# A cross-attention and mixture-of-experts layer on one core: the order of its tail laid out anew

## The chip, the cores and the metric

The kernel runs on one core of a Trainium2 chip. The metric is device time in microseconds (us) of one execution; lower is better. TensorE (PE) does matrix products and transposes, VectorE (DVE) and ScalarE (ACT) do elementwise work, GpSimd (POOL) does small work and issues the indirect DMAs, SyncE (SP) issues the other DMAs. Each engine runs its own list of instructions in order and waits on semaphores.

## What is computed

Two batches of 512 tokens of width 256, with a context of 1024 tokens each. First cross-attention with 16 heads, then a feed-forward layer made of a shared expert and eight routed experts, of which every token takes the best two.

```
x = x + attention(layernorm(x), ctx, ctx)           # W_Q, W_K, W_V, W_O, biases
xf = layernorm(x)
shared_out = silu(xf @ sw1) * (xf @ sw3) @ sw2       # 256 -> 512 -> 256
s = sigmoid(xf @ router_w.T)                         # 8 experts
topk_idx = top_k(s + router_bias, 2)                 # gates: s at the two, over their sum
routed_out = sum over the two of gate * gelu(xf @ ew1[e]) @ ew2[e]   # 256 -> 256 -> 256
out = x + shared_out + routed_out
```

## The kernel before, in words

One list, `steps`, is built in Python (line 84 on). TensorE, VectorE and ScalarE each walk the whole list and emit what a step asks of them, so the list is the order of the work on all three. SyncE and GpSimd have hand-written orders of their own. Products of float32 quality are made of three products of high and low parts (`product`, L1155), so an operand is split after each transpose: ScalarE copies the high part out of PSUM, VectorE subtracts it to get the low part.

Up to about 245 us the steps are attention units. The work on the routing of batch 0 (norm, transposes, logits, `router`, `choose`, `rank`, `place`, `gates`) is put beside the last units by `around_unit`. The tail begins behind them. What it holds, for batch b:

- Routing. `stats2`, `var2`, `norm2`: second layer norm (a first guess of 1/sqrt comes from GpSimd). `xpose2`: transposes of the normalised tokens. `logits`: 24 small matmuls. `router` (L916 to L923, with Exp on ScalarE at L851): sigmoid. `choose` (L930 to L938): the two best experts as one-hots, 12 small VectorE operations. `rank` (L1430 to L1434): matmuls that count tokens per expert. `place` (L992 to L1010): the row of each token in the sorted order (semaphore `pos_ready` at L1006), then the expert of each tile (`texp_ready` at L1010). `gates` (L943 to L956).
- Sorting. On GpSimd `sort_x(b)` (L693) writes the tokens into `xs_d` in HBM, sorted by expert: eight indirect DMAs. SyncE's `load_xs(b, i)` (L494) reads them back in pieces (`LOADS`), after all eight have landed.
- Expert tiles. 15 tiles of 128 rows, in 8 groups of two (the last of one). Groups are numbered q = 0 to 7 for batch 0 and 8 to 15 for batch 1. A group has four steps: `tx` (transposes of x, L1244; copies L782, L1033), `th` (12 matmuls with the first expert weights; Gelu L787), `tt` (transposes, L1265; copies L792, L1037), `ty` (12 matmuls with the second weights; copy to `ys`, L797). They form a pipeline: one round does `tx` of q, `th` of q-1, `tt` of q-2, `ty` of q-3. The results wait in a ring of `YR` buffers until GpSimd's `scatter_y(q)` (L698) has written them to their tokens in HBM (`ys_d`).
- Shared expert. `h` p = 0 to 3 for batch 0 and 4 to 7 for batch 1: 12 matmuls of 128x512 each, Silu on ScalarE (L773), three VectorE operations (L969, L975, L976). `y` (b, t), t = 0 to 3: 12 matmuls of 128x256 each; `add_y` (L982) adds the result to `x_sb`. `h`, `y`, `oproj`, `xpose2`, `logits` and `rank` take turns in two PSUM slots (the ring, `ring_at`).
- The end. SyncE loads the scattered results (L528, `yk`) when all of a batch have landed, `combine` (b, i) multiplies them with the gates and adds them (L1019), SyncE stores half a batch at a time (L532).

`with_group` says which routing and shared steps follow which round of the tiles. ScalarE's functions Exp, Silu and Gelu are in different tables; a switch shows as ACT_TABLE_LOAD. VectorE's routing operations are each followed by a wait on their own end (`link`).

Of the kernel before, what the change touches and what calls it, by code (L numbers as in the profile page):

```python
# [1479 lines left out]
```

## Time and profile before

| | |
|---|---|
| median of 3 runs | 373.58 us (371.82 to 375.38) |
| the profiled execution | 370.11 us, of which the span is 368.4 us |
| PE busy | 329.1 us (89%) |
| DVE busy | 260.7 us (71%) |
| ACT busy | 228.6 us (62%) |
| POOL busy | 150.2 us (41%) |
| chain that ended last, by engine | PE 66%, DVE 12%, DMA 7%, ACT 6%, issue 4%, POOL 2% |
| mean granted TensorE clock | 0.97 |

Busy time is the time in which an engine worked. The chain is followed back from the last instruction, at each step to what released it. The granted clock is the share of TensorE's full 2.4 GHz; half is 1.2 GHz. An interval in brackets behind a row is idle time of the engine before it, and what ended that.

### The profile page before, as it was taken

To read this page: it belongs to the slowest core of one execution; us is meant where nothing else is said; L and a number is where in the kernel's file an instruction comes from. 1 tells how busy PE (TensorE), PEld (TensorE's weight loads), DVE (VectorE), ACT (ScalarE), POOL (GpSimd) and SP (SyncE) were. 2 spreads that over 40 slices of the span, in tenths; PEclk is the share of its full clock that TensorE was granted. 3 is DMA by queue.
4 is the path that set the end of the run, shared out by engine and by line. 5 is a ranking of instruction groups with operands and counts; after the bars stand their busy time and mean duration, and the time that the engine had idled before them with its cause. 6 is when DMAs were issued, how large, how long until landed. Compare 5 with 4: busy or idle time off the path is not lost.

```text
span 368.4 us, 7264 instructions
## 1 busy us (share of the span) xinstructions
PE 329.1 (89%) x2636; PEld 202.5 (55%) x2636; DVE 260.7 (71%) x424; ACT 228.6 (62%) x408; POOL 150.2 (41%) x210
## 2 busy tenths in 40 slices
PE   5878998999999999999999999997999497599990
PEld 2665565333333333333643444467999495599880
DVE  6766988999999999999679538449642456355314
ACT  6452445898899899999568867631544352355710
POOL 5032479021063453466644645830131245515450
PEclk9998999999999999999999999999998899699997
DMA  7679990033160605436197050126020112663124
GB/s 287 255 247 347 303 371 9 2 112 126 43 196 6 217 21 158 138 86 210 28 322 204 19 163 3 56 73 204 3 101 26 47 45 86 200 217 142 59 73 171
DMA packets 29563, 49.52 MB, mean 134 GB/s; under 512 B 6404, under 2 KB 19844, under 8 KB 27844
## 3 DMA queue, kind: packets, MB, share of 16 engines
q1 hardware_dynamic: 27320, 43.02, 36.4%
q0 software_dynamic: 2208, 6.04, 4.6%
q8 instruction: 22, 0.36, 0.4%
q14 instruction: 13, 0.11, 0.1%
HBM read 29.00 MB, written 17.33 MB: 126 GB/s over the span
## 4 chain that ended last, share of the span: by engine, by line
PE 66%; DVE 12%; DMA 7%; ACT 6%; issue 4%; POOL 2%; SPq 1%; DVEq 0%; POOLq 0%; ACTq 0%
PE psum L1155 21%; PE psum L1334 18%; PE psum L1209 14%; PE psum L1215 7%; DVE negm L1046 3%; ACT PB L760 2%; PE psum L1244 2%; POOL xs_d L693 2%; PE psum L1265 2%; DMA VA<-xs_d 1%; DMA PB<-in_ctxT_dram 1%; SPq L425 1%; DMA PB<-ys_d 1%; DVE x_sb L1019 1%; DMA qs_d<-SWH 1%
## 5 line engine op out<-in xcount | busy, mean ns | idle before, releaser
L1046 DVE TENSOR_REDUCE negm<-psum 128x1 f32<-128x1024 f32 x128 | 153.7, 1222 | 13.9 <-PE psum L1215 13.3
L760 ACT ACTIVATE PB<-psum 128x512 f32<-128x512 f32 x256 | 138.4, 598 | 27.6 <-PE psum L1209 18.9
L1334 PE MATMUL psum<-PB,VA 128*17 128x256 f32 x1024 | 79.8, 385 | 2.8 <-ACT TMP L818 2.1
L1155 PE MATMUL psum<-EWT,WH 128*128 (+1 forms) x408 | 67.1, 316 | 2.0 <-DVE WH L1037 1.6
L1155 PEld LDWEIGHTS psum<-EWT,WH 128*128 128x128 f32 x408 | 57.2, 203 | 5.9 <-issue 4.1
L1209 PE MATMUL psum<-EWT 64*128 64x512 f32 x160 | 58.6, 449 | 0.4 <-ACT PB L760 0.2
L1215 PE MATMUL psum<-EWT 64*128 64x512 f32 x160 | 54.1, 457 | 4.4 <-DMA EWT<-qs_d 2.8
L698 POOL DMA_INDIRECT ys_d<-VA x30 | 28.9, 965 | 42.7 <-ACT VA L797 37.2
L1334 PEld LDWEIGHTS psum<-PB,VA 128*17 128x17 f32 x1024 | 17.4, 95 | 46.2 <-issue 34.8
L1209 PEld LDWEIGHTS psum<-EWT 64*128 64x128 f32 x160 | 24.5, 184 | 30.7 <-ACT PB L760 23.6
L1215 PE MATMUL psum<-S 64*128 64x512 f32 x96 | 32.2, 457 | 1.7 <-DVE negm L1046 1.1
L1209 PE MATMUL psum<-S 64*128 64x512 f32 x96 | 32.5, 463 | 0.0
L1215 PEld LDWEIGHTS psum<-EWT 64*128 64x128 f32 x160 | 22.0, 187 | 8.2 <-DMA EWT<-qs_d 3.0
L1155 PE MATMUL psum<-XT,SWH 128*128 128x512 f32 x96 | 25.0, 401 | 0.0
L782 ACT ACTIVATE WH<-psum 128x512 fp32r<-128x512 f32 (+1 forms) x16 | 9.1, 569 | 24.4 <-PE psum L1244 24.3
L1209 PEld LDWEIGHTS psum<-S 64*128 64x128 f32 x96 | 13.3, 184 | 17.8 <-ACT PB L760 13.9
L1037 DVE TENSOR_TENSOR WH<-psum,WH 128x512 fp32r<-128x512 f32 (+1 forms) x16 | 10.5, 658 | 16.4 <-ACT WH L792 16.4
L624 POOL TENSOR_TENSOR EWT<-RAW,EWT 128x512 fp32r<-128x512 f32 x16 | 20.6, 1288 | 1.3
L1155 PEld LDWEIGHTS psum<-XT,SWH 128*128 128x128 f32 x96 | 17.2, 188 | 6.3 <-issue 3.4
L797 ACT ACTIVATE VA<-psum 128x512 f32<-128x512 f32 (+1 forms) x16 | 9.1, 572 | 15.0 <-PE psum L1155 15.0
L787 ACT ACTIVATE RAW<-psum 128x512 f32<-128x512 f32 (+1 forms) x16 | 9.1, 571 | 12.3 <-PE psum L1155 12.2
L621 POOL TENSOR_SCALAR EWT<-RAW 128x512 fp32r<-128x512 f32 x16 | 9.9, 617 | 16.3 <-DMA RAW<-in_ew_dram 10.6
(189 smaller groups left out, 442.6 us busy)
## 6 DMA issues: line engine op xcount, KB each, us to landing
ks_d<-SWH SPq DMA_DIRECT2D x8, 512.0 KB, 4.4
RAW<-in_ew_dram SPq DMA_DIRECT2D x16, 256.0 KB, 3.0
xs_d<-VA SPq DMA_DIRECT2D x2, 1927.5 KB, 13.3
EWT<-ks_d SPq DMA_DIRECT2D x15, 256.0 KB
EWT<-qs_d SPq DMA_DIRECT2D x30, 128.0 KB
S<-ks_d SPq DMA_DIRECT2D x9, 256.0 KB
S<-qs_d SPq DMA_DIRECT2D x18, 128.0 KB
qs_d<-SWH SPq DMA_DIRECT2D x4, 512.0 KB, 4.8
```

The source lines that it names most:

```text
L621: pool.tensor_scalar(hi, RAW[:, c % 2, :], 1.0, 1.0, ALU.mult, ALU.mult).then_inc(pool_chain, 1)
L624: pool.tensor_tensor(lo, RAW[:, c % 2, :], raw(hi), ALU.subtract).then_inc(w_split, 1)
L698: pool.indirect_dma_start(ys_d[q // NGR], bass.IndirectOffsetOnAxis(sidx[:, q // NGR, i:i + 1], 0), ys[q % YR][:, j * D:(j + 1) * D], None ...
L760: act.activation(PB[:, n % PR, i * N:(i + 1) * N], bank[t % 3], ACT.Exp, scale=DK ** -0.5).then_inc(exp_done, 1)
L782: act.activation(xb[q % 2][0][:, 0:w], bank[0][:, 0:w], ACT.Copy).then_inc(x_hi, 1)
L787: act.activation(hs[q % 2][:, 0:w], bank[1][:, 0:w], ACT.Gelu).then_inc(gelu_done, 1)
L1037: dve.tensor_tensor(lo[:, 0:w], bank[2][:, 0:w], raw(hi[:, 0:w]), ALU.subtract).then_inc(h_lo, 1)
L1046: dve.tensor_reduce(negm[:, g % 2, r // QT, r % QT:r % QT + 1], psum[:, k0:k0 + 2, :].rearrange("p a n -> p (a n)"), AX.X, ALU.max, negate ...
L1155: r = pe.matmul(dst, a_hl[u], b_hl[v], start=first and i == 0, stop=last and i == 2)
L1209: pe.matmul(bank[t % 3], KS[s][rows, j, kp * P:(kp + 1) * P], QS[s][rows, j, :], start=True, stop=True).then_inc(scores_done, 1)
L1215: return pe.matmul(ring_bank(("max", m), half), QS[s][rows, j, qt * P:(qt + 1) * P], KS[s][rows, j, :], start=True, stop=True)
L1334: last = pe.matmul(acc[32 * j:32 * j + DK + 1, cols], VA[:, b, kp + KP * kk, GH * hg + j, :], PB[:, (4 * q + j) % PR, kk * N:(kk + 1) * N] ...
```

## The change

The tail's order is written out step by step instead of by `with_group`. The parts:

- `choose` and `place` are cut in two steps each, the last four operations of `place` become a step of their own (`experts`), and all of them are put between the tile steps of batch 0, `router` behind `add_y` and ahead of `th` 4. The logits of batch 1 are put between tile steps too. `norm2` of batch 1 comes ahead of `tx` 2 and `tt` 0.
- A step `exp_table` runs Exp on a scratch value ahead of the logits, so ScalarE changes tables there.
- `tx` 0 comes ahead of `oproj` and its wait for `oproj` is gone; `y` (0, 0) comes right behind `oproj`.
- `h` 7 goes from the eighth round of batch 1 to a place between `tx` 8 and `tx` 9; `h` 5 and `h` 6 follow `ty` 7.
- All four `y` of batch 1 come behind `ty` 15. Two used to stand between `ty` 14 and `ty` 15. `add_y` is cut in two halves; for batch 1 the second half comes behind both `combine`, and is the last operation.
- `combine` of batch 0 comes one round later.
- `LOADS`: four pieces instead of three, of 2, 2, 4 and 7 tiles. The loads of batch 1 wait until the low parts of x of batch 0 are made (`x_lo`), not until its results are scattered.
- `YR` 6 instead of 4; GpSimd scatters three groups ahead of `sort_x(1)` instead of four.

The same arithmetic is done. `choose` and `place` of batch 0 get the new cuts too.

```
@@ -40,10 +40,10 @@
-YR = 4
+YR = 6
...
-LOADS = ((0, 2), (2, XV), (XV, NTL))
+LOADS = ((0, 2), (2, 4), (4, XV), (XV, NTL))
...
-        for at, kind in ((18, "router"), (20, "choose"), (22, "rank"), (23, "place"), (25, "gates")):
+        for at, kind in ((18, ("router", 0)), (20, ("choose", 0, 0)), (20, ("choose", 0, 1)), (22, ("rank", 0)),
+                         (23, ("place", 0, 0)), (23, ("place", 0, 1)), (24, ("experts", 0)), (25, ("gates", 0))):
             if r == at:
-                todo += [(kind, 0)]
+                todo += [kind]
...
-    steps += [("sums", NG - 1), ("norm", NG - 1), ("oproj_part", 1), ("h", 2), ("h", 3), ("oproj", 1)]
-    with_group = {(0, 0): [("stats2", 1, t) for t in range(4)] + [("var2", 1)],
-                  (0, 1): [("y", 0, 0)], (0, 2): [("norm2", 1), ("y", 0, 1)], (0, 3): [("y", 0, 2), ("xpose2", 1)],
-                  (0, 4): [("y", 0, 3)] + [("logits", 1, t) for t in range(4)], (0, 5): [("router", 1)],
-                  (0, 6): [("choose", 1), ("rank", 1)], (0, 7): [("place", 1)], (0, 8): [("h", 4), ("gates", 1)],
-                  (0, 9): [("h", 5)], (0, 10): [("h", 6)],
-                  (1, 3): [("combine", 0, 0)], (1, 4): [("combine", 0, 1)], (1, 7): [("h", 7)],
-                  (1, 9): [("y", 1, 0), ("y", 1, 1)], (1, 10): [("y", 1, 2), ("y", 1, 3)]}
-    for b in range(B):
-        for i in range(NGR + 3):
-            steps += [(kind, NGR * b + i - d) for d, kind in enumerate(("tx", "th", "tt", "ty")) if 0 <= i - d < NGR]
-            steps += with_group.get((b, i), [])
-    steps += [("combine", 1, 0), ("combine", 1, 1)]
+    steps += [("sums", NG - 1), ("norm", NG - 1), ("oproj_part", 1), ("h", 2), ("h", 3), ("tx", 0), ("oproj", 1)]
+    steps += [("y", 0, 0), ("th", 0)] + [("stats2", 1, t) for t in range(4)] + [("var2", 1)]
+    steps += [("tx", 1), ("y", 0, 1), ("th", 1), ("norm2", 1), ("tx", 2), ("tt", 0), ("y", 0, 2)]
+    steps += [("th", 2), ("tx", 3), ("xpose2", 1), ("tt", 1), ("y", 0, 3), ("ty", 0), ("th", 3), ("exp_table",)]
+    steps += [("logits", 1, 0), ("tx", 4), ("logits", 1, 1), ("tt", 2), ("logits", 1, 2), ("ty", 1), ("add_y", 0, 0)]
+    steps += [("add_y", 0, 1), ("logits", 1, 3), ("router", 1), ("th", 4), ("choose", 1, 0), ("tx", 5), ("choose", 1, 1)]
+    steps += [("tt", 3), ("ty", 2), ("th", 5), ("rank", 1), ("place", 1, 0), ("tx", 6), ("place", 1, 1), ("tt", 4)]
+    steps += [("ty", 3), ("th", 6), ("tx", 7), ("tt", 5), ("ty", 4), ("experts", 1), ("th", 7), ("tt", 6), ("ty", 5)]
+    steps += [("h", 4), ("tt", 7), ("ty", 6), ("ty", 7), ("gates", 1), ("h", 5), ("h", 6)]
+    steps += [("tx", NGR), ("h", 7), ("tx", NGR + 1), ("th", NGR)]
+    for i in range(2, NGR + 3):
+        q = NGR + i
+        for kind, r in (("tx", q), ("th", q - 1), ("tt", q - 2), ("ty", q - 3)):
+            if NGR <= r < 2 * NGR:
+                steps.append((kind, r))
+        if i in (4, 5):
+            steps.append(("combine", 0, i - 4))
+    steps += [("y", 1, 0), ("y", 1, 1), ("add_y", 1, 0), ("combine", 1, 0), ("y", 1, 2), ("y", 1, 3)]
+    steps += [("combine", 1, 1), ("add_y", 1, 1)]
...
-        ys = [va[1][:, i * N:(i + 1) * N] for i in range(YR)]
+        ys = [va[1][:, i * N:(i + 1) * N] for i in range(4)] + [TMP[:, i, :] for i in range(2)]
...
-                    for q in range(lo // 2, (hi + 1) // 2):
-                        sp.wait_ge(ys_stored[q % YR], ys_count(q))
+                    sp.wait_ge(x_lo, (hi + 1) // 2)
...
-                for q in range(NGR * b + NGR - YR, NGR * b + NGR):
+                for q in range(max(0, NGR * b + NGR - YR), NGR * b + NGR):
...
-            for q in range(4):
+            for q in range(3):
                 scatter_y(q)
             sort_x(1)
-            for q in range(4, 2 * NGR):
+            for q in range(3, 2 * NGR):
...
-                    elif q == 0:
-                        act.wait_ge(ring_full, ring_at[("oproj", 1)] + 1)
...
+                elif st[0] == "exp_table":
+                    act.activation(exp_in[:, :], exp_in[:, :], ACT.Exp)
...
-            def add_y(tb):
-                ring_wait(("y", tb))
-                for t in range(4):
-                    src = ring_bank(("y", tb), t // 2)[:, (t % 2) * D:(t % 2 + 1) * D]
+            def add_y(tb, half):
+                if half:
+                    ring_wait(("y", tb))
+                else:
+                    dve.wait_ge(y_half, tb + 1)
+                for t in range(2 * half, 2 * half + 2):
+                    src = ring_bank(("y", tb), half)[:, (t % 2) * D:(t % 2 + 1) * D]
                     dst = x_sb[:, 4 * tb + t, :]
                     last = dve.tensor_tensor(dst, src, dst, ALU.add)
-                last.then_inc(slot_empty(("y", tb)), 1)
-                dve.wait_ge(*freed(("y", tb)))
-            def place(b):
+                if half and tb:
+                    last.then_inc(combined, 1)
+                elif half:
+                    last.then_inc(slot_empty(("y", tb)), 1)
+                    dve.wait_ge(*freed(("y", tb)))
+                else:
+                    link(last)
...
-                    if k == 0:
+                    if k == 0 or (b, i) == (1, 1):
                         link(last)
-                last.then_inc(combined, 1)
+                if (b, i) != (1, 1):
+                    last.then_inc(combined, 1)
...
-                    if t == 3:
+                    if t == 1:
+                        r.then_inc(y_half, 1)
+                    elif t == 3:
```

On VectorE, at the router of batch 1 (`xn` holds the routing's small tiles here, `WH` a tile's low part): before.

```order
L1031 TENSOR_TENSOR VA<-PB,spare 128x2
L1033 TENSOR_TENSOR WH<-psum,WH 128x512
L1037 TENSOR_TENSOR WH<-psum,WH 128x512
L916 COPY xn<-psum 128x32
L918 COPY rs<-xn 128x1
L921 TENSOR_SCALAR xn<-xn 128x32
L922 RECIPROCAL xn<-xn 128x32
L923 TENSOR_TENSOR xn<-xn,rows 128x32
L1031 TENSOR_TENSOR VA<-PB,spare 128x2
L1033 TENSOR_TENSOR WH<-psum,WH 128x512
L1037 TENSOR_TENSOR WH<-psum,WH 128x512
L930 TENSOR_REDUCE rs<-xn 128x4
```

The same place after the change (L923 is now the copy out of PSUM, L1056 a tile's low part).

```order
L994 TENSOR_TENSOR x_sb<-psum,x_sb 128x256 x4
L923 COPY xn<-psum 128x32
L925 COPY rs<-xn 128x1
L928 TENSOR_SCALAR xn<-xn 128x32
L929 RECIPROCAL xn<-xn 128x32
L930 TENSOR_TENSOR xn<-xn,rows 128x32
L937 TENSOR_REDUCE rs<-xn 128x4
L938 TENSOR_TENSOR xn<-xn,rs 128x32
L939 TENSOR_TENSOR xn<-xn,desc 128x32
L940 TENSOR_REDUCE rs<-xn 128x4
L941 TENSOR_TENSOR xn<-xn,rs 128x32
L944 SCALAR_TENSOR_TENSOR xn<-xn 128x32
```

Before, the router's copy stood behind the low parts of `tx` 5 and `tt` 3, and the choice behind those of `tx` 6 and `tt` 4. After, both follow the logits directly, and the low part of `tx` 5 comes behind the first half of the choice.

On TensorE, where batch 0 ends and batch 1 begins: before (12 matmuls of 128x512 are one `h`, here `h` 6).

```order
L1155 MATMUL psum<-EWT,WH 128x256 x2
L1155 MATMUL psum<-XT,SWH 128x512 x12
L1225 TENSOR_LOAD VA
L1244 MATMUL psum<-ident,VA 128x128 x4
L1225 TENSOR_LOAD VA
```

After: `h` 5 and `h` 6, `tx` 8, `h` 7, `tx` 9.

```order
L1180 MATMUL psum<-XT,SWH 128x512 x24
L1250 TENSOR_LOAD VA
L1269 MATMUL psum<-ident,VA 128x128 x4
L1180 MATMUL psum<-XT,SWH 128x512 x12
L1250 TENSOR_LOAD VA
L1269 MATMUL psum<-ident,VA 128x128 x4
```

`h` 7 now stands between the first two transposes of batch 1; it was some 30 us further down.

On VectorE, the end of the program: before.

```order
L1037 TENSOR_TENSOR WH<-psum,WH 128x512
L1037 TENSOR_TENSOR WH<-psum,WH 128x256
L982 TENSOR_TENSOR x_sb<-psum,x_sb 128x256 x4
L1019 SCALAR_TENSOR_TENSOR x_sb<-PB,VA,x_sb 128x256 x8
L179 UNCONDITIONAL_BRANCH
```

After.

```order
L1060 TENSOR_TENSOR WH<-psum,WH 128x256
L994 TENSOR_TENSOR x_sb<-psum,x_sb 128x256 x2
L1041 SCALAR_TENSOR_TENSOR x_sb<-PB,VA,x_sb 128x256 x8
L994 TENSOR_TENSOR x_sb<-psum,x_sb 128x256 x2
L186 UNCONDITIONAL_BRANCH
```

Two of the four additions of the shared expert's result moved behind the combination.

## Rows read from the trace of the kernel before

**Rows 1.** The page: span, and the granted TensorE clock in 40 slices.

```profile
span 368.4 us, 7264 instructions
PEclk9998999999999999999999999999998899699997
```

**Rows 2.** Windows: length, busy per engine (PE, PEld, DVE, ACT, POOL), PEclk, DMA share, GB/s.

```profile
277.00:283.00 6.00, 6.00 (x40) 6.00 (x40) 1.70 (x5) 1.91 (x4) 0.00 (x0) 0.72 0.07 25
...
312.00:323.00 11.00, 5.54 (x26) 4.86 (x26) 3.33 (x7) 4.00 (x6) 5.93 (x7) 0.69 0.63 186
```

**Rows 3.** Timeline of TensorE, steady stretch: start, duration, line, [idle before <- releaser].

```profile
263.51 0.60 PE L1244 MATMUL psum<-ident,VA 128*128 128x128 f32 x4
263.86 1.68 PE L1155 MATMUL psum<-EWT,WH 128*128 x12
265.38 0.60 PE L1265 MATMUL psum<-ident,RAW 128*128 128x128 f32 x4
265.74 1.67 PE L1155 MATMUL psum<-EWT,WH 128*128 x12
267.25 1.60 PE L1155 MATMUL psum<-SWH,S 128*128 128x256 f32 x12
268.69 1.04 PE L1373 MATMUL psum<-ident,xn 128*128 128x128 f32 x8
```

**Rows 4.** Timeline of TensorE: its waits in the tail, and its slow steps.

```profile
256.43 0.63 PE L1244 MATMUL psum<-ident,VA 128*128 128x128 f32 x4 [1.87 <-DVE WH L1033]
...
277.76 2.75 PE L1155 MATMUL psum<-EWT,WH 128*128 x12
...
291.33 0.19 PE L1430 MATMUL psum<-VA,lower 128*128 128x8 bf16 x2 [4.75 <-DVE VA L938]
...
292.06 2.91 PE L1155 MATMUL psum<-EWT,WH 128*128 x12
...
308.30 0.98 PE L1155 MATMUL psum<-EWT,WH 128*128 x6 [1.63 <-DVE WH L1037]
...
315.31 0.99 PE L1244 MATMUL psum<-ident,VA 128*128 128x128 f32 x4 [3.27 <-DMA VA<-xs_d]
318.30 1.11 PE L1244 MATMUL psum<-ident,VA 128*128 128x128 f32 x4 [1.99 <-DMA VA<-xs_d]
319.06 2.91 PE L1155 MATMUL psum<-EWT,WH 128*128 x12
...
350.17 0.41 PE L1265 MATMUL psum<-ident,RAW 128*128 128x128 f32 x2 [1.11 <-DVE WH L1037]
...
355.55 3.04 PE L1155 MATMUL psum<-SWH,S 128*128 128x256 f32 x24
```

**Rows 5.** Timeline of VectorE: the router's copy, and the end of `place`.

```profile
282.64 0.18 DVE L916 COPY xn<-psum 128x32 f32<-128x32 f32 x1
...
298.69 0.17 DVE L1006 CAST VA<-xn 128x8 int32<-128x8 f32 x1
```

**Rows 6.** Timeline of ScalarE: the load of the Exp table.

```profile
283.50 1.28 ACT L851 ACT_TABLE_LOAD   x1
```

**Rows 7.** Timeline of GpSimd: first and last scatter of the sort, the last results.

```profile
299.14 0.96 POOL L693 DMA_INDIRECT xs_d<-xn,VA  x1 [8.00 <-DVE VA L1006]
...
309.90 0.96 POOL L693 DMA_INDIRECT xs_d<-PB,VA  x1 [2.20 <-issue]
...
356.40 0.96 POOL L698 DMA_INDIRECT ys_d<-VA  x1 [1.16 <-ACT VA L797]
```

**Rows 8.** Chain of waits in order of time, its end: start, duration, what.

```profile
356.40 2.40 DMA ys_d<-VA
...
358.94 3.35 DMA PB<-ys_d
```

**Rows 9.** Timeline of VectorE: the last additions and the combination of batch 1.

```profile
358.62 1.42 DVE L982 TENSOR_TENSOR x_sb<-psum,x_sb 128x256 f32<-128x256 f32 x4 [7.16 <-PE psum L1155]
362.39 3.51 DVE L1019 SCALAR_TENSOR_TENSOR x_sb<-PB,VA,x_sb 128x256 f32<-128x256 f32 x8 [2.35 <-DMA PB<-ys_d]
```

More of the change, by code:

```diff
@@ L355, in xattn_ffn @@
         combined = sem("combined")
+        y_half = sem("y_half")
         x_turned = sem("x_turned")
@@ L923, in route, with choose @@
                 link(dve.tensor_tensor(sel_, s_, bc(rbv), ALU.add))
-            def choose(b):
-                if b == 0:
+            def choose(b, k):
+                if b == 0 and k == 0:
                     dve.wait_ge(pv_done, 4 * HG * KP)
@@ L934, in first_max @@
                     link(dve.tensor_tensor(oh, w_, bc(per_token(b, 1)), ALU.is_equal))
-                first_max(oh)
-                link(dve.scalar_tensor_tensor(out=sel_, in0=oh, scalar=-1e30, in1=sel_, op0=ALU.mult, op1=ALU.add))
-                first_max(oh2)
-                dve.tensor_tensor(both_b[:, :, :], oh, oh2, ALU.add).then_inc(both_ready, 1)
+                if k == 0:
+                    first_max(oh)
+                    link(dve.scalar_tensor_tensor(out=sel_, in0=oh, scalar=-1e30, in1=sel_, op0=ALU.mult, op1=ALU.add))
+                else:
+                    first_max(oh2)
+                    dve.tensor_tensor(both_b[:, :, :], oh, oh2, ALU.add).then_inc(both_ready, 1)
             def gates(b):
@@ new lines, in add_y, with cube @@
+                if half and tb:
[3 more added lines that the diff above has]
+                    dve.wait_ge(*freed(("y", tb)))
+                else:
+                    link(last)
+            last1 = lambda v, n: v.rearrange("p (a o) -> p a o", o=1).broadcast_to([P, v.shape[1], n])
+            mid1 = lambda v, n: v.rearrange("p (o a) -> p o a", o=1).broadcast_to([P, n, v.shape[1]])
+            def cube(b, lo, a, n):
+                return work[b][:, lo:lo + a * n].rearrange("p (a n) -> p a n", n=n)
@@ new lines, in place @@
+            def place(b, part):
+                w = work[b]
+                tiles, first, rk, base = w[:, 320:328], w[:, 328:336], w[:, 344:384], w[:, 480:512]
+                if part == 0:
+                    if b == 0:
+                        dve.wait_ge(order_consts, 15)
+                    ring_wait(("rank", b))
+                    dve.tensor_copy(rk, ring_bank(("rank", b))[:, 0:40]).then_inc(slot_empty(("rank", b)), 1)
+                    dve.wait_ge(*freed(("rank", b)))
+                    link(dve.tensor_tensor(cube(b, 384, NE, 4), last1(rk[:, 32:40], 4), mid1(steps128[:, :], NE), ALU.is_gt))
+                    link(dve.tensor_reduce(tiles, cube(b, 384, NE, 4), AX.X, ALU.add))
+                    link(dve.tensor_tensor(cube(b, 416, NE, NE), before[:, :, :], mid1(tiles, NE), ALU.mult))
+                    link(dve.tensor_reduce(first, cube(b, 416, NE, NE), AX.X, ALU.add))
+                else:
+                    link(dve.scalar_tensor_tensor(out=base.rearrange("p (t e) -> p t e", e=NE), in0=mid1(first, 4),
+                                                  scalar=float(P), in1=rk[:, 0:32].rearrange("p (t e) -> p t e", e=NE),
+                                                  op0=ALU.mult, op1=ALU.add))
+                    link(dve.tensor_tensor(cube(b, 0, 2, 4 * NE), chosen(b), twice(base), ALU.mult))
+                    link(dve.tensor_reduce(tiles_f(b), cube(b, 0, 8, NE), AX.X, ALU.add))
+                    dve.tensor_copy(pos[:, b, :], tiles_f(b)).then_inc(pos_ready, 1)
@@ L1007, in place, with experts @@
+            def experts(b):
+                w = work[b]
+                tiles, first, ends, over = w[:, 320:328], w[:, 328:336], w[:, 336:344], w[:, 464:464 + NTL]
                 link(dve.tensor_tensor(ends, first, tiles, ALU.add))
-                link(dve.tensor_tensor(cube(344, NTL, NE), last1(column[:, 0:NTL], NE), mid1(ends, NTL), ALU.is_ge))
-                link(dve.tensor_reduce(w[:, 464:464 + NTL], cube(344, NTL, NE), AX.X, ALU.add))
-                dve.tensor_scalar(texp[:, b, :], w[:, 464:464 + NTL], float(NE - 1), float(EXPERT), ALU.min, ALU.mult)\
+                link(dve.tensor_tensor(cube(b, 344, NTL, NE), last1(column[:, 0:NTL], NE), mid1(ends, NTL), ALU.is_ge))
+                link(dve.tensor_reduce(over, cube(b, 344, NTL, NE), AX.X, ALU.add))
+                dve.tensor_scalar(texp[:, b, :], over, float(NE - 1), float(EXPERT), ALU.min, ALU.mult)\
@@ L1138, in _ @@
                     hidden(st[1])
-                elif st[0] == "y" and st[2] == 3:
-                    add_y(st[1])
+                elif st[0] == "add_y":
+                    add_y(*st[1:])
                 elif st[0] == "choose":
-                    choose(st[1])
+                    choose(*st[1:])
                 elif st[0] == "place":
-                    place(st[1])
+                    place(*st[1:])
+                elif st[0] == "experts":
+                    experts(st[1])
                 elif st[0] == "gates":
```

20 lines of the change are left out of this document (removed).

## The prediction

> **What bounds the kernel now.** I read the page first. Over most of the 368.4 us span the granted clock stands at nine tenths or more; it dips only in slices near 280, 295 and 315 us [rows 1]. Up to about 255 us the change touches nothing but the cut of batch 0's routing, so the question lies in the last 115 us. There the timeline of TensorE is an almost unbroken row of steps, and the end follows its pace wherever it is unbroken. From starts that follow each other, a step costs at full clock: `tx` 0.35 us (263.51 to 263.86), `th` 1.52, `tt` 0.36, `ty` 1.51, `y` 1.44 [rows 3]. What isn't work is in the idle times of the same timeline [rows 4]: 1.87 (VectorE's low part of `tx` 0), 4.75 (`rank` waits for the choice), 1.63 (`ty` 7 waits for a low part behind the gates), 3.27 and 1.99 (the first two loads of batch 1), 1.11 (`tt` 15). The third thing is slow steps: `th` 4, `th` 6 and `th` 8 take 2.75, 2.91 and 2.91 us where 1.68 is the rule [rows 3, 4]; in 277 to 283 us and in 312 to 323 us the granted clock is 0.72 and 0.69 [rows 2], that is, part of these stretches ran at 1.2 GHz. The last two dips follow TensorE's waits; the first follows the 24 tiny logits matmuls.
>
> Why the loads are late is one chain. The router's copy on VectorE runs at 282.64 although the logits end near 277.5, for it stands behind two tile steps [rows 5]. Exp then waits for a table load of 1.28 [rows 6]. Choice, rank and place follow, each behind further tile steps, and the positions are there at 298.87 [rows 5]. The sort takes from 299.14 to 310.86 on GpSimd [rows 7], and batch 1's first transpose starts at 315.31 [rows 4]: 16.4 us after the positions. While this goes on TensorE runs out of batch 0.
>
> **The change, part by part.** I walk TensorE through the new list with the prices above.
>
> *Start.* `tx` 0 ahead of `oproj` makes no time: `y` (0, 0) now stands behind `oproj` and needs its slot, which VectorE frees by the same additions as before. The wait is again about 1.9 us, ending near 256.4, and `tx` 0, `tx` 1, `th` 0, `y` (0, 0) are done at about 259.8 in both. From there to the end of the logits the list holds the same steps in another order; with VectorE's part in it I find one wait of 0.3 (`th` 1 for its low part, `y` (0, 1) doesn't cover it whole). So the logits end at 277.7, as before within 0.4.
>
> *Routing of batch 1.* The copy goes from 282.64 to 277.8. Router: 1.4 us instead of 3.2, the Exp table being there since `exp_table`. Twelve operations of the choice at 0.22 each are 2.7, the low part of `tx` 5 between them 0.85 and its wait 0.25: 282.9. `rank` 0.6, five operations of `place` at 0.23 1.2, low part of `tx` 6 0.8, four operations 0.9: the positions at 286.4, 12.5 us earlier than 298.87. On TensorE this costs short waits, as the low parts of `tx` 5 and `tx` 6 come late behind a half of the choice or of `place`: 0.2 for `th` 5, 0.1 for `th` 6. Without such cover the dearest piece is 1.3. The 4.75 go, since `th` 4, `tx` 5, `tt` 3, `ty` 2 and `th` 5 now lie between logits and `rank`.
>
> A rule bears on this. The trace shows 1.28 for a table load and the function right behind it [rows 6]. The Trainium skill (ScalarE: Activation LUTs, What ACT_TABLE_LOAD costs) adds a drain of about 1.38 to each switch. By the rule the Gelu table's load behind the router's Exp would hold back `th` 4's Gelu, and with it `tx` 5's copy and `rank`, 1.4 us longer; the sum below would be 1.4 us less good. I go by the row.
>
> *Sort and loads.* GpSimd has its three groups scattered by 284.7. With 16.4 from positions to landed data, the first piece lands at 302.9. When is TensorE there? It reached `tx` 8 at 315.31; minus waits of 4.75 + 1.63 + 3.27, minus slow steps of about 4.0 ahead of it, plus waits of its own (0.3 + 0.2 + 0.1, and 1.4 for `ty` 7, whose low part is behind `h` 4's three operations on VectorE), plus 0.8 for a clock that still dips: 304.5. So the load is 1.6 us early and TensorE isn't held. The second piece, now two tiles, is covered by `h` 7: the 1.99 go. Nearest rows for the other pieces: 8 tiles took some 5.4 us before; the last seven are wanted 10 us after `tx` 8.
>
> *Clock.* Twelve-matmul steps lose 1.07, 1.23 and 1.23 [rows 3, 4]; the transposes beside them 0.39 and 0.5 (0.99 and 1.11 against 0.60), further small ones about 1.1: 5.5 in all, 4.0 ahead of `th` 8, 1.5 from it on. Two of the three dips follow waits that go. For the one behind the logits I keep half, 0.8: they are as tiny as before (the bound 1.6), but tile steps stand between them (the bound 0).
>
> *Batch 1.* New waits: 0.3 before `tx` 9 and 1.25 before `tx` 10 (the low part of `tx` 9 stands behind `h` 7's 1.8 us on VectorE), 0.65 before `ty` 15, which needs `ty` 14's PSUM bank copied out and has no `y` in between any more. Gone: 0.2, the 1.11, one table pair, and two `y`, 2.88, from ahead of `ty` 15. `h` 7 itself is only moved.
>
> *End.* Before, the last group's scatter starts at 356.40, lands 2.40 later, `yk` takes 3.35 [rows 8], the combination 3.51 [rows 9], and the span ends 2.5 later. After, groups 13, 14 and 15 leave TensorE faster than GpSimd issues (1.27 per tile), so the last scatter starts 2.1 late against `ty` 15. The four `y` take 5.8 behind `ty` 15 and hide in the 9 us of scatter and load. The second `add_y` half is now last on VectorE: half of 1.42, 0.7 [rows 9].
>
> *Nothing.* Six `ys` buffers, the later `combine` and the split `place` of batch 0: `ty` never waited for a buffer, and batch 0's routing has tens of microseconds to spare. `yk` of batch 0 needs nine scatters behind the sort (to 309.8, landed 312, loaded 316), and VectorE wants it at 322.
>
> **Sum.** Waits gone 4.75 + 1.63 + 3.27 + 1.99 + 0.2 + 1.11 = 12.95; clock 5.5; two `y` 2.9: 21.3. Against it waits 0.3 + 0.2 + 0.1 + 1.4 + 0.3 + 1.25 + 0.65 = 4.2, clock 0.8, end 2.8: 7.8. Net 13.5 less: span 354.9, with the 1.7 around it 356.6. The profiled execution (370.11) lies 3.5 under the median 373.58; carried over, 360.1. I say 360.
>
> **Rivals.**
> 1. *The waits go but the clock doesn't come back.* For: the first dip began in a stretch without a wait [rows 2]. Against: 323 to 343 us ran full, and new waits are below 1.9, like the one at 256.43, after which steps were at full speed [rows 3, 4]. Then 4.7 of the sum are missing: 364.8. The Trainium skill (TensorE: Matmul & The Clock Gate, The HAM clock gate) calls the slow phase run-variable and advises against fitting a count to it. By this the 4.7 I credit are the least safe term. The trace agrees in that its three dips have no common length.
> 2. *Transfers replace waits.* The first load, or batch 0's `yk`, comes late: the sort, the backlog of nine scatters and 2 MB of loads now run close together, and `combine` (0, 0) holds VectorE and so TensorE. For: the slack of the first load is only 1.6. Against: the same mix ran in 312 to 323 us with DMA at 0.63 [rows 2]. A loss of 4: 364.
> 3. *Better than walked.* Waits are half of mine, the clock stays up, the end's queue is hidden: 3.5 more, 356.5.
> 4. *The routing pieces starve TensorE* (the other side). It happens between 278 and 287 us: every piece on VectorE holds a low part, TensorE idles in each round, and the clock halves the 12 us of work there. Price: 6 of waits, 6 of clock, and the first load late by as much, 3: within 1%, 371 to 375. It turns into a loss only if the positions come after about 303, that is 16 us later than walked; for that VectorE, 5 us busy in 10 there, would have to be full twice over.
>
> That the change doesn't do what it says is excluded by the instruction order.
>
> **Chances.** Forecast 0.60, clock 0.12, transfers 0.12, better 0.11, starving 0.05 (of it slower 0.02). The forecast's own range is 356.5 to 363.5, from new waits between 2 and 6, the dip 0 to 1.6, and the median's offset between 2 and 5. To hold 8 in 10 I reach over rivals 1 and 2 and part of 3: 355 to 366.5. A difference below 1% can't be told from none here. Faster by over 1%: 0.95, within 0.03, slower 0.02.
>
> **What would show it.** Positions near 286 us and the sort's first scatter right behind; `tx` 8 without idle time before it, near 304.5; `h` 7, then `tx` 9 at once; `rank` without its 4.75; `th` 6 and `th` 8 at 1.68; `ty` 15 ending near 338; the last scatter 3 us after it, queued behind its neighbours; `add_y` last. Wrong if `tx` 8 waits for a load, if `th` 4 to `th` 8 stay near 2.9, or if the end after `ty` 15 takes more than 17 us.

## The result and the profile after

The changed kernel takes 359.65 us (median of 4 runs, 356.12 to 361.89) against 372.98 us before in the same job: ratio 0.960, 95% interval 0.951 to 0.970. The prediction said 360 and kept 355 to 366.5. The profiled execution took 356.12 us with a span of 354.3 us; the sum had said 356.6 and 354.9. With the later jobs there are 16 executions of the changed kernel, from 355.4 to 364.6, median 360.7. The ratios leave out executions that lie more than 1.5% above the fastest of their kernel; medians are over all executions.

The page of the changed kernel: the span, and the clock in 40 slices, which has no dip before the last slice, against [rows 1].

```profile
span 354.3 us, 7265 instructions
PEclk9999999999999999999999999999999999999996
```

The timeline of TensorE, its waits in the tail and the steps around them. L1180 is now the product helper, L1269 `tx`, L1290 `tt`.

```profile
255.89 1.69 PE L1180 MATMUL psum<-SWH,S 128*128 128x256 f32 x12 [1.81 <-DVE x_sb L1158]
...
261.08 1.69 PE L1180 MATMUL psum<-EWT,WH 128*128 x12 [0.19 <-DVE WH L1056]
...
277.40 1.68 PE L1180 MATMUL psum<-EWT,WH 128*128 x12
...
282.07 1.69 PE L1180 MATMUL psum<-EWT,WH 128*128 x12 [0.68 <-DVE WH L1056]
...
298.68 0.98 PE L1180 MATMUL psum<-EWT,WH 128*128 x6 [1.37 <-DVE WH L1060]
299.49 5.61 PE L1180 MATMUL psum<-XT,SWH 128*128 128x512 f32 x24
304.94 0.60 PE L1269 MATMUL psum<-ident,VA 128*128 128x128 f32 x4
305.30 2.99 PE L1180 MATMUL psum<-XT,SWH 128*128 128x512 f32 x12
308.47 0.63 PE L1269 MATMUL psum<-ident,VA 128*128 128x128 f32 x4 [0.18 <-DVE WH L1056]
308.85 1.67 PE L1180 MATMUL psum<-EWT,WH 128*128 x12
311.65 0.63 PE L1269 MATMUL psum<-ident,VA 128*128 128x128 f32 x4 [1.13 <-DVE WH L1056]
...
336.34 1.69 PE L1180 MATMUL psum<-EWT,WH 128*128 x12 [0.40 <-ACT VA L802]
338.90 0.98 PE L1180 MATMUL psum<-EWT,WH 128*128 x6 [0.88 <-ACT VA L802]
339.72 5.91 PE L1180 MATMUL psum<-SWH,S 128*128 128x256 f32 x48
```

The 4.75 before `rank`, the 3.27 and 1.99 before the two loads, and the slow steps of 2.75 and 2.91 [rows 4] are gone: `th` 4 (277.40) takes 1.68 and `th` 8 (308.85) 1.67. `tx` 8 starts at 304.94 right behind `h` 6, ten microseconds earlier than the 315.31 of before.

The timeline of VectorE: the router's copy and the end of `place`, against [rows 5].

```profile
278.22 0.19 DVE L923 COPY xn<-psum 128x32 f32<-128x32 f32 x1
...
287.03 0.17 DVE L1025 CAST VA<-xn 128x8 int32<-128x8 f32 x1
```

The timeline of GpSimd: first and last scatter of the sort, the first scatter of group 14, the last scatter of all, against [rows 7]. And the end of the chain of waits, against [rows 8].

```profile
287.73 0.97 POOL L700 DMA_INDIRECT xs_d<-xn,VA  x1 [3.17 <-DVE VA L1025]
...
298.34 0.97 POOL L700 DMA_INDIRECT xs_d<-PB,VA  x1 [2.06 <-issue]
...
338.93 0.96 POOL L705 DMA_INDIRECT ys_d<-VA  x1 [0.33 <-ACT VA L802]
...
341.46 0.96 POOL L705 DMA_INDIRECT ys_d<-VA  x1 [0.30 <-issue]
```

```profile
341.46 2.40 DMA ys_d<-VA
...
344.01 3.40 DMA PB<-ys_d
```

The positions come 11.7 us earlier and the sort follows them at once. Take the start of the first step behind the wait for the `oproj` additions on VectorE (255.89; before it is 256.43 [rows 4], where the low part of `tx` 0, behind the additions, ends the wait). From there to the end of the span there were 112.0 us, now 98.4: 13.6 less. The other 0.5 fell ahead of the tail.

The executions of one kernel differ by several microseconds with the mean granted clock: the changed kernel's lie between a span of 353.7 at 0.991 and 362.9 at 0.961. A single profile is therefore compared from a point behind its dips. The measure below is **th 1 to end**, from the start of `th` 1 of batch 0 to the end of the span. It is 93.2 in the changed kernel (354.3 less 261.08), and 93.3 and 93.5 in two more profiles of it. It can't be read finer than about 0.5: the load of `yk` near the end alone takes 3.4 to 4.0 in the profiles of the changed kernel and its variants, though no edit touches it.

Five of the experiments have only two executions each (medians 360.94 for the two `y`, 367.35 for the ring of four, 360.85 without `exp_table`, 365.24 for the logits, 359.01 for three loads). That is too few to settle differences of 1 to 4 us, so they are read by their profiles, one each.

### The profile page after: what moved, and what is told of

Read it like the earlier page. It is cut to its first block, busy times and chain, and to the rows that moved or that the text cites. A ratio compares the mean times of both kernels' runs of the same rounds, so it can differ in the third digit from the quotient of the medians.

```text
span 354.3 us, 7265 instructions
## 1 busy us (share of the span) xinstructions
PE 322.7 (91%) x2636; PEld 196.3 (55%) x2636; DVE 260.8 (74%) x424; ACT 226.0 (64%) x407; POOL 150.8 (43%) x210
## 4 chain that ended last, share of the span: by engine, by line
PE 66%; DVE 16%; ACT 6%; DMA 6%; issue 3%; SPq 1%; POOL 1%; DVEq 0%; POOLq 0%; ACTq 0%
PE psum L1180 23%; PE psum L1359 17%; PE psum L1234 13%; PE psum L1240 7%; DVE negm L1069 6%; ACT PB L767 2%; DMA PB<-in_ctxT_dram 2%; PE psum L1290 1%; PE psum L1269 1%; DVE PB L978 1%; DMA EWT<-qs_d 1%; DVE S L985 1%; DMA PB<-ys_d 1%; DVE x_sb L1041 1%; DMA qs_d<-SWH 1%
## 5 line engine op out<-in xcount | busy, mean ns | idle before, releaser
L1180 PE MATMUL psum<-EWT,WH 128*128 (+1 forms) x408 | 62.4, 302 | 4.5 <-DVE WH L1060 1.4
L1180 PEld LDWEIGHTS psum<-EWT,WH 128*128 128x128 f32 x408 | 53.3, 190 | 8.9 <-issue 7.4
L1359 PEld LDWEIGHTS psum<-PB,VA 128*17 128x17 f32 x1024 | 17.4, 95 | 46.2 <-issue 34.9
L705 POOL DMA_INDIRECT ys_d<-VA x22 | 21.4, 973 | 30.3 <-ACT VA L802 26.0
L1180 PE MATMUL psum<-XT,SWH 128*128 128x512 f32 x96 | 24.9, 401 | 0.0
L1234 PEld LDWEIGHTS psum<-S 64*128 64x128 f32 x96 | 13.3, 184 | 17.8 <-ACT PB L767 14.3
L1180 PEld LDWEIGHTS psum<-XT,SWH 128*128 128x128 f32 x96 | 17.2, 188 | 6.4 <-issue 3.4
L792 ACT ACTIVATE RAW<-psum 128x512 f32<-128x512 f32 (+1 forms) x16 | 9.1, 571 | 18.0 <-PE psum L1180 17.8
L571 POOL TENSOR_TENSOR rstd<-ve,mhalf 128x4 f32<-128x4 f32 x4 | 4.6, 1152 | 28.6 <-DVE ve L876 28.6
L675 POOL TENSOR_TENSOR TMP<-TMP 128x512 f32<-128x512 f32 x6 | 7.7, 1281 | 20.1 <-ACT TMP L837 20.1
```

What stands on the lines that cost most here:

```text
L675: pool.tensor_tensor(RC, U[g % 2], RC, ALU.mult).then_inc(rc_scaled, 1)
L705: pool.indirect_dma_start(ys_d[q // NGR], bass.IndirectOffsetOnAxis(sidx[:, q // NGR, i:i + 1], 0), ys[q % YR][:, j * D:(j + 1) * D], None ...
L792: act.activation(hs[q % 2][:, 0:w], bank[1][:, 0:w], ACT.Gelu).then_inc(gelu_done, 1)
L1180: r = pe.matmul(dst, a_hl[u], b_hl[v], start=first and i == 0, stop=last and i == 2)
L1234: pe.matmul(bank[t % 3], KS[s][rows, j, kp * P:(kp + 1) * P], QS[s][rows, j, :], start=True, stop=True).then_inc(scores_done, 1)
L1359: last = pe.matmul(acc[32 * j:32 * j + DK + 1, cols], VA[:, b, kp + KP * kk, GH * hg + j, :], PB[:, (4 * q + j) % PR, kk * N:(kk + 1) * N] ...
```

## The experiments

### The routing put back late

```
-    ... ("th", 3), ("exp_table",)]
-    ... ("logits", 1, 3), ("router", 1), ("th", 4), ("choose", 1, 0), ("tx", 5), ("choose", 1, 1)]
-    [("tt", 3), ("ty", 2), ("th", 5), ("rank", 1), ("place", 1, 0), ("tx", 6), ("place", 1, 1), ("tt", 4)]
-    [("ty", 3), ("th", 6), ("tx", 7), ("tt", 5), ("ty", 4), ("experts", 1), ...
+    ... ("th", 3)]
+    ... ("logits", 1, 3), ("th", 4), ("tx", 5)]
+    [("tt", 3), ("ty", 2), ("router", 1), ("th", 5), ("tx", 6), ("tt", 4)]
+    [("ty", 3), ("choose", 1, 0), ("choose", 1, 1), ("rank", 1), ("th", 6), ("tx", 7), ("tt", 5), ("ty", 4)]
+    [("place", 1, 0), ("place", 1, 1), ("experts", 1), ...
```

> The changed kernel with the routing pieces of batch 1 put back: router behind ty 2, the whole choice and rank behind ty 3, the whole place behind ty 4, no exp_table. All else is as changed. Theory (the early positions carry the gain): the positions come at about 298 us instead of 287.2, rank waits some 4 to 5 us again, tx 8 waits for its load until about 314.5 instead of starting at 304.9, and the dips of the granted clock come back. Span about 10 to 12 above the changed kernel's 354.3, so 364 to 366. Rival (the gain is in h 7, the y order and the loads, the routing only moves waits about): below 358.

Median 371.84 us (10 runs) against 373.54 before in the same job, ratio 0.994 (0.989 to 1.000). Its profiled execution has a span of 372.4 us at clock 0.96. Most of the excess over 364 to 366 lies ahead of the tail: `th` 1 starts at 266.65. From `th` 1 to the end it takes 105.7, that is 12.5 more than the changed kernel, where the theory had 10 to 12. The timeline of TensorE:

```profile
295.70 0.20 PE L1458 MATMUL psum<-VA,lower 128*128 128x8 bf16 x2 [4.80 <-DVE VA L948]
...
296.07 2.91 PE L1181 MATMUL psum<-EWT,WH 128*128 x12
...
321.34 0.66 PE L1270 MATMUL psum<-ident,VA 128*128 128x128 f32 x4 [4.13 <-DMA VA<-xs_d]
321.75 4.58 PE L1181 MATMUL psum<-XT,SWH 128*128 128x512 f32 x12
```

The wait of `rank`, the wait for the load and the slow steps behind each are back. All the other edits together, without the early routing, leave 1.7 us between the medians, a difference below 1%; behind the wait for the additions they leave 110.9 (372.4 less 261.46) against 112.0. The rival that the gain is in them falls. That doesn't make them worthless: with the early routing in place, `h` 7 and the buffers are worth 3.9 and 2.6 (below). No run has the early routing without the other edits, so what it gives by itself is not shown.

### The same kernel with its two long waits filled

```
+                    if b == 1:                       # in rank, ahead of the wait for both_ready
+                        for _ in range(20):
+                            pe.matmul(o[:, :], identb[:, :], RU[:, :].bitcast(BF16)[:, 0:N], ...)
...
+                    if q == NGR:                     # in tx, ahead of the wait for xs_loaded
+                        for _ in range(18):
+                            pe.matmul(bank[0], identb[:, :], RU[:, :].bitcast(BF16)[:, 0:N], ...)
```

> The kernel with the routing put back late (the first experiment), whose rank waits 4.80 us and whose tx 8 waits 4.13 us, with 20 and 18 dummy matmuls of 128x512 (their result is overwritten) in those two waits; nothing else differs. It leaves the waits and takes away the idle time in them. Theory (the idle time in a wait costs a second time, because TensorE's clock falls behind it): th 6 takes 1.68 instead of 2.91 and h 7 2.9 instead of 4.58; the granted clock from 277 to 345 us stays at 1.0; from the start of y (0,0) to the end 110.9 become about 107.5. Rival (the slow steps have another cause): unchanged within 0.5.

```profile
293.37 4.49 PE L1461 MATMUL psum<-RU,identb 128*128 128x512 bf16 x20
...
298.62 1.68 PE L1181 MATMUL psum<-EWT,WH 128*128 x12
...
317.04 4.06 PE L1266 MATMUL psum<-RU,identb 128*128 128x512 bf16 x18
321.07 0.66 PE L1273 MATMUL psum<-ident,VA 128*128 128x128 f32 x4
321.49 2.99 PE L1181 MATMUL psum<-XT,SWH 128*128 128x512 f32 x12
```

With TensorE busy in the waits, `th` 6 takes 1.68 instead of 2.91 and `h` 7 2.99 instead of 4.58; the granted clock from 277 to 345 us is 1.0. From the start of `y` (0, 0) 107.8 remain of 110.9: 3.2 less, where about 3.4 was expected. A dip behind `y` (0, 0), which the other execution didn't have, is in the 107.8; from `th` 1 to the end 101.1 remain of 105.7. So 8.9 us of waits cost 4.6 more by what followed them. These slow steps come from the idle time ahead of them: 4.1 of the 4.6 lie between `rank` and `ty` 7 (2.5) and between `tx` 8 and `tx` 9 (1.6). Another 0.3 is a load that holds TensorE less, as the quicker steps let `place` come earlier. The medians are 370.26 (9 runs) and 371.84 for the kernel without fillers in the other job, beside medians of before of 374.42 and 373.54; they don't settle it.

### h 7 back in its late round

```
-    steps += [("tx", NGR), ("h", 7), ("tx", NGR + 1), ("th", NGR)]
+    steps += [("tx", NGR), ("tx", NGR + 1), ("th", NGR)]
...
+        if i == 7:
+            steps.append(("h", 7))
```

> The changed kernel with h 7 back in the eighth round of batch 1, behind ty 12. Theory (h 7 only fills a hole of about 1.4 us between tx 8 and tx 9, and itself delays the low part of tx 9): th 8 starts 1.9 earlier, tx 10 no longer waits (1.1 gained), then 2.8 are given back by h 7 and 1.1 by the wait of tt 15 behind the change of tables: 0.8 slower, span about 355.1. Rival (the place of h 7 is worth its whole 2.8): span 357 to 358.

`th` 1 to end is 97.1, 3.9 more; median 365.66 (4 runs) against 360.75 (6 runs) for the changed kernel in the same job. My theory (0.8) missed this widely and the rival's 2.8 was nearer. The timeline:

```profile
313.57 0.63 PE L1271 MATMUL psum<-ident,VA 128*128 128x128 f32 x4 [2.92 <-DVE WH L1058]
...
316.13 1.05 PE L1271 MATMUL psum<-ident,VA 128*128 128x128 f32 x4
```

`tx` 9 starts 3.52 behind `tx` 8 here (310.05) and 3.53 in the changed kernel: the low part of `tx` 8 stands behind the three VectorE operations of `h` 6, with or without `h` 7. The hole is 2.92 us, not 1.4, and `h` 7 fills all of it. Without it the clock falls behind the hole (the transposes of `tx` 10 take 1.05), which eats what the missing wait of `tx` 10 would give. Later come `h` 7's own 2.8 and the 1.11 before `tt` 15.

### Two y of batch 1 back between ty 14 and ty 15

```
+        if i == NGR + 1:
+            steps += [("y", 1, 0), ("y", 1, 1)]
```

> The changed kernel with y (1,0) and y (1,1) back between ty 14 and ty 15; the additions stay in two halves. Theory (the 2.9 us of two y ahead of ty 15 were mostly hidden, because GpSimd would be issuing the scatters of groups 13 and 14 meanwhile): ty 15 ends 2.0 later, since its wait of 0.88 for the bank goes, and the last scatter starts 0.8 behind it instead of 1.8: about 0.95 slower from ty 14 to the end. Rival (the order is worth its 2.9): 2.9 slower. Read from the start of ty 14 to the end of the span, which a dip of the clock elsewhere does not touch: 18.0 in the changed kernel.

From the start of `ty` 14 (338.91) to the end of the span (357.7) 18.8, against 18.0 (354.3 less 336.34): 0.8 more. The theory had 0.95, the rival 2.9. The last scatter, on the timeline of GpSimd, now waits for ScalarE and isn't queued:

```profile
344.89 0.96 POOL L707 DMA_INDIRECT ys_d<-VA  x1 [1.16 <-ACT VA L804]
```

So the 2.9 that the sum gave to the moved `y` and the 2.8 that it charged to the end belong together.

### A ring of four buffers

```
-YR = 6
+YR = 4
```

> The changed kernel with a ring of four result buffers instead of six, still three groups scattered ahead of the sort. Theory (buffers are worth next to nothing): the copy of ty 7 waits for the scatter of group 3 behind the sort, until about 303.3 instead of 299.7, but h 5 and h 6 cover it on TensorE; the low part of tx 8 comes 0.3 to 0.6 later, span plus 0.3 to 0.6. Rival (ScalarE's wait holds up h 5 and so h 7's slot): 3 us more before tx 9.

`th` 1 to end is 95.8, 2.6 more. ScalarE and then TensorE:

```profile
309.82 0.38 ACT L802 ACTIVATE VA<-psum 128x256 f32<-128x256 f32 x1 [7.44 <-DMA ys_d<-VA]
```

```profile
311.54 3.04 PE L1180 MATMUL psum<-XT,SWH 128*128 128x512 f32 x12 [1.55 <-DVE PB L978]
```

The copy of `ty` 7 waits for the scatter of group 3, which is now behind the sort, and lands 2 us later than I had reckoned (309.82 is 49.5 behind `y` (0, 0), or 305.4 on the changed kernel's scale, not 303.3). Silu for `h` 5 stands behind it, and `h` 7 waits for the slot. The rival holds: with the new order the two added buffers are worth 2.6 us.

### No exp_table, and the price of a table switch

```
-    ... ("ty", 0), ("th", 3), ("exp_table",)]
+    ... ("ty", 0), ("th", 3)]
```

> The changed kernel without the exp_table step. Theory: the table load starts when ty 1's copy ends at 277.6 and is over at 278.9, so the router's Exp comes 0.45 later than 278.44; the Gelu, the copy of tx 5, the wait of th 5 (0.68) and the positions all come 0.5 later: 0.5 slower. Rival (by the Trainium skill, ScalarE: Activation LUTs, What ACT_TABLE_LOAD costs, each switch has a drain of about 1.38 beside the load): the Exp comes 1.8 later.

`th` 1 to end is 94.2, 1.0 more, of which 0.5 are the wait of `th` 5 (1.16 instead of 0.68), as expected; the other 0.5 lie between the last scatter and the start of `combine` (6.5 instead of 6.05), which the step can't touch. ScalarE:

```profile
281.27 1.28 ACT L856 ACT_TABLE_LOAD   x1
282.57 0.23 ACT L856 ACTIVATE xn<-xn 128x32 f32<-128x32 f32 x1
282.82 1.28 ACT L792 ACT_TABLE_LOAD   x1
284.11 0.60 ACT L792 ACTIVATE RAW<-psum 128x512 f32<-128x512 f32 x1
```

The load starts 0.01 behind the activation before it (which ends at 281.26), and the function 0.02 behind the load, twice in a row. The Exp comes 17.8 behind `th` 1 instead of 17.4, so 0.5 later and not 1.8. The Trainium skill (ScalarE: Activation LUTs, What ACT_TABLE_LOAD costs) adds a drain of about 1.38 to each load of about 1.28. This trace doesn't agree: only the 1.28 show.

### The logits in one piece

```
-    [("logits", 1, 0), ("tx", 4), ("logits", 1, 1), ("tt", 2), ("logits", 1, 2), ("ty", 1), ("add_y", 0, 0)]
-    [("add_y", 0, 1), ("logits", 1, 3), ("router", 1), ...
+    [("tx", 4), ("tt", 2), ("ty", 1), ("add_y", 0, 0)]
+    [("add_y", 0, 1)] + [("logits", 1, t) for t in range(4)] + [("router", 1), ...
```

> The changed kernel with the 24 logits matmuls of batch 1 in one piece behind ty 1, as they stood before. Theory A (a run of tiny matmuls makes the clock dip): th 4 takes 2.7 us instead of 1.68, the granted clock in the 6 us behind the logits is near 0.7, and the span is about 1.5 longer. Theory B (only waits make it dip, the one of before was chance): th 4 takes 1.68 and the span is the same within 0.3.

```profile
283.61 2.74 PE L1180 MATMUL psum<-rw,XT 128*128 128x8 f32 x24
...
287.74 1.06 PE L1269 MATMUL psum<-ident,PB 128*128 128x128 f32 x4
...
289.30 3.91 PE L1180 MATMUL psum<-EWT,WH 128*128 x24
```

A dip is there, one step later than I had said: `th` 4 takes 1.73, but the transposes behind it 1.06 and 24 product matmuls 3.91 instead of 3.04, with no wait ahead of them. `th` 1 to end is 94.2, 1.0 more. None of the profiles with the logits spread has a dip at this place. The wait of 0.68 before `th` 5 is gone, which hides a part of the dip. All this fits theory A in kind; one profile doesn't settle its size. Nor are four pieces a sure remedy. The 24 logits matmuls of batch 0 stand in four pieces of 6 between attention steps near 210 us in every kernel, and there the granted clock falls to 0.5 within 6 us of the start of the first piece in 4 of the 14 profiles (this one, the filled waits, and the last two below), with no wait above 0.25 in the 10 us ahead. The ten others show no dip there. What decides between them is open.

### Three loads instead of four

```
-LOADS = ((0, 2), (2, 4), (4, XV), (XV, NTL))
+LOADS = ((0, 2), (2, XV), (XV, NTL))
```

> The changed kernel with three loads per batch (2, 6 and 7 tiles) instead of four. Theory (h 7 covers the second load): tx 9 keeps its wait of 0.18 for a low part, no wait for a load anywhere, the same within 0.5 from y (0,0) to the end (98.4). Rival (the second load of six tiles lands 5.4 us after its issue, which would be 306.3 in the changed kernel, and later still with the backlog of scatters): tx 9 waits, 1 to 2 us slower.

```profile
312.14 0.63 PE L1269 MATMUL psum<-ident,VA 128*128 128x128 f32 x4 [0.17 <-DVE WH L1056]
```

`tx` 9 has the same short wait for VectorE and none for a load. `th` 1 to end is 93.6, the same within 0.5. The smaller second load is worth nothing that shows here.

### The addition early and tt 7 ahead of h 4

```
-    steps += [("h", 4), ("tt", 7), ("ty", 6), ("ty", 7), ...
+    steps += [("tt", 7), ("h", 4), ("ty", 6), ("ty", 7), ...
-    [("y", 1, 0), ("y", 1, 1), ("add_y", 1, 0), ("combine", 1, 0), ("y", 1, 2), ("y", 1, 3)]
-    [("combine", 1, 1), ("add_y", 1, 1)]
+    [("y", 1, 0), ("y", 1, 1), ("add_y", 1, 0), ("y", 1, 2), ("y", 1, 3), ("add_y", 1, 1)]
+    [("combine", 1, 0), ("combine", 1, 1)]
```

> The changed kernel with two edits: the last add_y half ahead of both combinations, and tt 7 ahead of h 4. Theory: the shared result is ready at about 345.5, the scattered rows at 347.5, so the addition hides: 0.75 less at the end. The low part of tt 7 no longer stands behind the three VectorE operations of h 4: the wait of 1.37 before ty 7 goes, and the load of batch 1 (landed near 303.8) allows 1.2 of it: together 1.9 less, span 352.4. Rival (the end is set by GpSimd's scatters of groups 13 to 15 alone): the wait that goes turns up before tx 8 as a wait for the load, and only 0.75 are left.

```profile
255.50 2.75 PE L1177 MATMUL psum<-SWH,S 128*128 128x256 f32 x12 [1.80 <-DVE x_sb L1155]
...
299.58 0.98 PE L1177 MATMUL psum<-EWT,WH 128*128 x6 [0.88 <-ACT VA L802]
```

`th` 1 to end is 92.5, 0.7 less, which is little more than the measure can tell. The wait of `ty` 7 doesn't go: it becomes 0.88 for the copy of `ty` 6 out of the bank, which the old wait had hidden. Since `tt` 7 now starts 0.2 late, only 0.2 are won from `th` 1 to `h` 5 (38.2 against 38.4). The rest comes from the early addition: from `ty` 15 to the end 14.85 instead of 15.40. The rival had the amount right, but its reason, a wait for the load before `tx` 8, doesn't appear. Medians can't tell the two kernels apart: 361.14 (6 runs) against 360.75 for the changed kernel in the same job. The first row shows `y` (0, 0) at 2.75 instead of 1.69, behind the same wait of 1.8.

> The changed kernel itself, in the same job as the others. Theory: span 354 with the granted clock at 0.99, and 3 to 6 us more where the clock dips. The difference between executions is the clock's: about 3.5 us per 0.012 of its mean.

Its spans there were 354.1 and 355.0 at clock 0.991, 358.6 and 359.3 at 0.98, 360.9 at 0.967 and 361.5 at 0.971. The first step down, of 0.011, costs 4.4, the next, of 0.013, only 2.0; over both that is 3.2 per 0.012, so the 3.5 hold roughly.

### Fillers in two waits

```
+            def filler(dst, n):
+                for _ in range(n):
+                    pe.matmul(dst, ident[:, :].bitcast(BF16)[:, 0:P], RU[:, :].bitcast(BF16)[:, 0:N], ...)
...
+                    if m == 0:
+                        filler(ring_bank(("max", 0), 1), 13)
...
+                    if (tb, t) == (0, 0):
+                        filler(bank[1], 8)
```

> The version with the early addition and tt 7 ahead of h 4, and with dummy matmuls in two waits: 13 in the 3.1 us in which the first maxima wait for their stack near 25 us, 8 in the 1.8 us ahead of y (0,0). Theory (the executions of one kernel differ by the clock's dips, and the first one follows the 3.1 us wait): the granted clock near 30 us stays at 1.0 in every profile, and the median comes 1 to 3 us below the changed kernel's of the same job. Rival (the dips near 30 and 70 us come from the thin stretch of maxima, not from the wait): no difference, or as much slower as the fillers overrun their waits.

> The changed kernel itself beside the fillers. Theory: median 360 to 361, executions between 355 and 363 along the clock's mean of 0.99 to 0.967.

Median 358.12 us (6 runs, 355.20 to 359.61) against 362.11 for the changed kernel in the same job (6 runs, 355.40 to 364.60), which is above the 360 to 361 expected for it. The ratios to before, 0.956 (0.951 to 0.960) and 0.957 (0.949 to 0.965), are alike, and so are the best executions. The mean clocks are 0.978 to 0.994 against 0.961 to 0.991. The stretch from 27 to 36 us by windows (columns as in [rows 2]), first of the changed kernel in this job, then of the kernel with fillers:

```profile
27.00:36.00 9.00, 7.39 (x36) 5.44 (x36) 5.34 (x6) 1.69 (x3) 2.98 (x2) 0.81 0.99 355
```

```profile
27.00:36.00 9.00, 8.20 (x45) 4.89 (x43) 6.11 (x7) 2.23 (x5) 3.59 (x2) 1.00 1.00 356
```

The dip is gone here, but it is missing in two profiles of the changed kernel as well, so one profile proves little. The pages show a larger one elsewhere, first without and then with the fillers; a slice is 9 us.

```profile
PEclk9998999999999999999999965899989999999997
```

```profile
PEclk9999999999999999999999985999999999999996
```

In both the clock falls near 212 us, at the logits of batch 0, where neither filler stands. From the first of these logits to `tx` 0 it is 48.4 us without and 46.3 with the fillers, against 42.2 in the first profile of the changed kernel: 6.1 of the 8.6 us between that profile (354.3) and this one (362.9) arise there. So the larger part of this gap isn't in the waits that were filled. Whether the fillers make the kernel faster or its executions more alike is not shown; the 4.0 between the medians is no gain to count on.

## Why the prediction held, point by point

- **The start.** As said: a wait of 1.81 for the `oproj` additions, 0.19 before `th` 1 (0.3 said), no gain from `tx` 0.
- **Routing.** The router's copy at 278.22 (277.8 said), the positions at 287.2 (286.4). The logits end at 277.5 as said, but the copy stands behind `add_y`, which VectorE finishes at 278.2; this 0.4 was missed, and everything up to the positions carries it. The wait of `th` 5 is 0.68, not 0.2. Of the 0.5 more, 0.4 is the same delay. The other 0.1 is in the wait of the low part of `tx` 5 for its copy on ScalarE, 0.33 instead of 0.25, as Gelu and the copy stand behind the table load that follows Exp.
- **Sort and load.** `tx` 8 at 304.94 (304.5), without a wait. How much earlier the load had landed the trace doesn't show. The slack was put at 1.6 by 16.4 from positions to data; the experiment with late routing had 17.7 from the positions (303.6) to `tx` 8, which would leave nothing. Counted from the start of the last scatter of the sort, `tx` 8 came 5.4 later before, 6.1 with late routing, both times held by the load, and 6.6 in the changed kernel. By that the load was 0.5 to 1.2 early: an estimate, and less than the 1.6.
- **Waits.** Said 4.2 in sum, measured 0.19 + 0.68 + 0.15 + 1.37 + 0.18 + 1.13 + 0.40 + 0.88 = 5.0. The largest miss is `th` 5. The working also missed the 0.40 before `ty` 14, which like the 0.88 before `ty` 15 is a wait for the PSUM bank.
- **Clock.** Said 5.5 won and 0.8 kept. The logits dip did not stay at all in this profile. The account 12.95 - 5.0 + clock + 2.9 - end has to give 13.6. With 1.8 for the end, the clock's term is 4.5: by difference about 1 less than summed from the steps. That the slow steps behind `rank` and the load are the price of idle time is shown by the filled waits. One argument failed, though: rival 1 was answered with the wait of 1.87, after which the steps ran at full speed. The same wait of 1.8 to 1.9 is followed by slow steps in 5 of the 13 profiles that have it unfilled, at a cost of about 1.5 each time (6.7 instead of 5.2 from `y` (0, 0) to `th` 1). No new wait was followed by slow steps in any profile of the changed kernel; the longest is 1.37.
- **End.** Said 2.8 longer. From the start of `ty` 15 to the end it takes 15.4 (338.90) against 13.6 (354.82, the row below): 1.8. Of this 1.0 lies ahead of the last scatter and 0.8 behind it. The scatter's queue was over-sized, since the bank waits slow TensorE to GpSimd's pace: group 14 isn't queued, only the last tile is, and it loses 1.0 and not 2.1. The late addition costs what was said, 0.7; the version without it is 0.55 shorter from `ty` 15 to the end. `ty` 15 itself ended at 339.9, 1.9 later than said, and the last scatter started 1.6 behind it and not 3.

```profile
354.82 0.88 PE L1155 MATMUL psum<-EWT,WH 128*128 x6
```

- **"Nothing".** This part was wrong in one point. Six buffers were called free because `ty` never waited for one. That was true of the old order, where group 3 was scattered ahead of the sort. The same change moves it behind the sort, and there the ring of four costs 2.6 us. `combine` and `yk` were rightly priced at nothing: `yk` of batch 0 was issued at 312.5, and `combine` started at 321.8 without waiting for it.
- **The median.** The offset of 3.5 between profile and median was carried over from before and was 3.5 again. It is the clock's dips elsewhere, which each kernel's executions have or don't have. The profiled execution of the changed kernel was one of its fastest, without any dip up to the end, so the 356.1 beside the 356.6 of the sum owes something to luck, and so does the equal offset.

The errors were small and of both signs: waits 0.8 more, clock 1.0 less won and 0.8 less kept, end 1.0 less. The mechanism is as predicted. That the sum meets the tail's 13.6 within 0.1 is because these errors cancel, which is luck.

## What to carry to other kernels

Find the chain that fills the next stage's data and see on every engine what stands ahead of its links; here small VectorE operations stood behind tile steps that weren't urgent, and putting them first moved 11.7 us. Price an idle wait on TensorE at more than its length if the work behind it is dense. Check each buffer count against the new order, not against the waits of the old trace.
